# Four GNN layers on one Trainium2 core: a new order on DVE, ACT and GpSimd inside the steps of layers 2 and 3

## What is computed

```python
x = _layernorm(x + L0(x, adj))            # graph convolution with two batch norms
x = _layernorm(x + L1(x, edges))          # attention over 256 edges, 4 heads
x = _layernorm(x + L2(x, adj, adj))       # three weighted convolutions
x = _layernorm(x + L3(x, adj))            # attention over all pairs of nodes

def _slconv(x, adj, S, W):                # layer 2: weighting = adj * adj
    return einsum('nm,bmh->bnh', adj * S, einsum('bnf,fh->bnh', x, W))
# L2: h = relu(slconv(x, W1)); h = relu(slconv(h, W2)); slconv(h, W3)     128 -> 256 -> 512 -> 128

def L3(h, adj):
    Wh = h @ W
    e = (Wh @ a1)[:, :, None] + (Wh @ a2)[:, None, :]
    e = where(e >= 0, e, 0.2 * e)                         # leaky ReLU
    e = where(adj == 0, -inf, e)
    return softmax(e, -1) @ Wh
```

## Time and profile before

| | us |
|---|---|
| median of 3 runs | 638.22 (638.16 to 639.72) |
| the profiled execution | 637.05 |
| its span | 635.1 |
| PE busy | 553.0 (87%) |
| DVE busy | 422.8 (67%) |
| ACT busy | 367.1 (58%) |
| POOL busy | 217.7 (34%) |
| mean granted TensorE clock | 0.93 of 2.4 GHz |

### The profile page before, as it was taken

One profiled execution on the slowest core, in us unless ns is written; L12 is line 12 of the kernel. 1 busy time (PEld: TensorE's weight loads), 2 busy tenths in 40 slices (PEclk: granted clock), 3 DMA queues, 4 the chain that ended last, 5 costly groups with the idle time before them and its releaser, 6 DMA issues.

```text
span 635.1 us, 11295 instructions
## 1 busy us (share of the span) xinstructions
PE 553.0 (87%) x3508; PEld 488.5 (77%) x3508; DVE 422.8 (67%) x1446; ACT 367.1 (58%) x733; POOL 217.7 (34%) x253
## 2 busy tenths in 40 slices
PE   2999797789998799998998999899799799799372
PEld 2888443568886798988988889889789789789262
DVE  5588586788882644685585575675675675755895
ACT  1566692576653245366666666666665765663660
POOL 6840520565663312314215215215215115103231
PEclk9999799699998799999899899799899899799777
DMA  5223000321100000000001001000000000100002
GB/s 178 87 79 99 2 0 0 98 57 45 33 1 0 2 1 1 1 1 1 1 2 35 0 1 33 0 0 23 10 0 12 22 0 1 33 1 9 26 2 66
DMA packets 28382, 15.25 MB, mean 24 GB/s; under 512 B 2320, under 2 KB 28048, under 8 KB 28352
## 3 DMA queue, kind: packets, MB, share of 16 engines
q1 hardware_dynamic: 27792, 13.65, 7.5%
q0 software_dynamic: 560, 1.25, 0.5%
HBM read 10.69 MB, written 4.19 MB: 23 GB/s over the span
## 4 chain that ended last, share of the span: by engine, by line
PE 71%; DVE 12%; ACT 9%; issue 4%; POOL 2%; DMA 1%; SPq 1%; DVEq 0%; ACTq 0%; POOLq 0%
PE psum L237 13%; PE psum L238 12%; PE psum L239 12%; PE psum L1496 8%; PE psum L1321 5%; PE psum L1363 4%; ACT soft L1178 4%; ACT ob L231 3%; PE psum L1448 2%; PE psum L1370 2%; PE psum L1374 2%; PE psum L1384 2%; PE psum L1438 2%; DVE ln_st L183 2%; PE psum L1542 2%
## 5 line engine op out<-in xcount | busy, mean ns | idle before, releaser
L202 POOL TENSOR_TENSOR ln_r<-ln_v,mhalf 128x8 f32<-128x8 f32 x32 | 53.8, 1681 | 257.6 <-DVE ln_v L196 257.6
L1496 PE MATMUL psum<-l2w_s,h 128*128 128x128 f32 x512 | 59.7, 275 | 0.0
L1496 PEld LDWEIGHTS psum<-l2w_s,h 128*128 128x128 f32 x512 | 59.0, 192 | 0.7
L1165 ACT ACTIVATE h<-psum 128x512 f32<-128x512 f32 x64 | 37.3, 596 | 33.4 <-PE psum L239 33.4
L237 PE MATMUL psum<-qt_hi,l2w_s_hi 128*128 128x512 f32 x128 | 52.6, 411 | 0.0
L238 PE MATMUL psum<-qt_lo,l2w_s_hi 128*128 128x512 f32 x128 | 50.5, 394 | 0.0
L239 PE MATMUL psum<-qt_hi,l2w_s_lo 128*128 128x512 f32 x128 | 50.5, 394 | 0.0
L231 ACT ACTIVATE keep_x<-keep_x,ln_b,ln_r (+1 forms) x112 | 45.9, 483 | 1.4 <-POOL ln_b L205 1.4
L854 DVE TENSOR_TENSOR s_lo<-psum,s_hi 128x512 fp32r<-128x512 f32 x16 | 11.1, 692 | 47.5 <-ACT s_hi L1169 47.5
L183 DVE BATCH_NORM_STATS2 ln_st<-keep_x 128x6 f32<-128x128 f32 (+1 forms) x192 | 39.1, 277 | 2.9 <-ACT keep_x L1092 1.6
L237 PE MATMUL psum<-l2w_s_hi,pt_hi 128*128 128x256 f32 x64 | 22.4, 350 | 19.6 <-DVE pt_lo L839 19.6
(11 more groups left out here) (225 smaller groups left out, 1824.9 us busy)
## 6 DMA issues: line engine op xcount, KB each, us to landing
xin<-in_x SPq DMA_DIRECT2D x64, 128.0 KB, 2.2
out_x<-ob SPq DMA_DIRECT2D x32, 128.0 KB, 1.8
l2w_raw<-in_l2w POOLq DMA_DIRECT2D x1, 512.0 KB, 6.7
adjs<-in_adj SPq DMA_DIRECT2D x1, 256.0 KB, 2.7
adjs<-in_adj_t SPq DMA_DIRECT2D x1, 256.0 KB, 2.9
l2w_s<-in_l2w POOLq DMA_DIRECT2D x1, 256.0 KB, 6.5
w_raw<-in_w_t SPq DMA_DIRECT2D x1, 128.0 KB, 3.2
w2t<-in_w_t SPq DMA_DIRECT2D x1, 128.0 KB, 3.2
```

Of the source, the lines that this page charges most:

```text
L202: pool.tensor_tensor(ln.r[:].rearrange("p s k -> p (s k)"), ln.v[:].rearrange("p s k -> p (s k)"), mhalf[:], ALU.pow).then_inc(ln.root, 1)
L1165: act.activation(h2[:, s, g, :], bank(4 + g)[:, 0, :], ACT.Relu).then_inc(h2_out, 1)
L1496: i = pe.matmul(bank(s)[:, 0, k * D:(k + 1) * D], h2[:, s, g, j * N + t * P:j * N + (t + 1) * P], l2w3_s[:, g, :], start=(g == 0), stop=(g ...
```

## The change

No instruction is added or taken away, and PE and SP are untouched. Inside `step`, and in DVE's tail, the order is another:

- POOL: `weigh` comes first, then the roots of ln2 and ln1, then `split_x3(p-1)`, both `split_x(p+1)`, and the root of ln3 last.
- DVE: `variance(p-1, ln2)` moves behind both `h1_low` and the first addition of layer 1; `variance(p+1, ln1)` ahead of `turned_low`; the eight maxima of `scores3` between the two `s3_low`; the three small steps become `highest`, behind the second `s3_low`; both additions of layer 2 follow, and only then `leaky3` of slot 0. `leaky3` of slot 1 comes in the next step, behind both `pt_low`.
- ACT: `exps` moves from ahead of `h1_high` to ahead of `qt_high`; the scalings of ln2 move in between the ReLUs of `h2`; those of ln1 come ahead of the last two ReLUs of slot 1; those of ln3 ahead of `s3_high(p, 1)`.

```diff
             def step(p, two_ahead=True, ahead=True, behind=True, two_behind=True):      # POOL
-                if behind:
-                    ln_power(pool, p - 1, ln2)
                 if two_ahead:
                     for s in range(2):
                         weigh(s, 2 * (p + 2) + s, False)
+                if behind:
+                    ln_power(pool, p - 1, ln2)
                 if ahead:
                     ln_power(pool, p + 1, ln1)
+                if behind:
+                    split_x3(p - 1, not two_behind)
                 if ahead:
                     split_x(p + 1, 0, False)
+                    split_x(p + 1, 1, False)
                 if two_behind:
                     ln_power(pool, p - 2, ln3)
-                if ahead:
-                    split_x(p + 1, 1, False)
-                if behind:
-                    split_x3(p - 1, not two_behind)
...
+            def highest(p):                                                             # DVE
                 dve.wait_ge(tm_done, 2 * p + 2)
...
-            def leaky3(p):
-                for s in range(2):
-                    dve.wait_ge(zt_ready, 2 * p + s + 1)
+            def leaky3(p, s):
+                dve.wait_ge(zt_ready, 2 * p + s + 1)
...
                 for s in range(2):
                     pt_low(p, s)
+                if two_behind:
+                    leaky3(p - 2, 1)
+                for s in range(2):
+                    h1_low(p, s)
+                if ahead:
+                    add(p + 1, 0, o1_done, 4, ln1)
                 if behind:
                     variance(p - 1, ln2, not two_behind)
-                for s in range(2):
-                    h1_low(p, s)
-                for s in range(2):
-                    if ahead:
-                        add(p + 1, s, o1_done, 4 + s, ln1)
-                    qt_low(p, s)
+                qt_low(p, 0)
+                if ahead:
+                    add(p + 1, 1, o1_done, 5, ln1)
+                qt_low(p, 1)
...
+                if ahead:
+                    variance(p + 1, ln1, False)
                 if two_behind:
                     turned_low(p - 2)
                     weights3(p - 2, layer2_first(p))
-                if ahead:
-                    variance(p + 1, ln1, False)
...
+                if behind:
+                    scores3(p - 1)
                 s3_low(p, 1)
                 if behind:
-                    scores3(p - 1)
-                    leaky3(p - 1)
+                    highest(p - 1)
                 for s in range(2):
                     add(p, s, o2_done, 2 + s, ln2)
+                if behind:
+                    leaky3(p - 1, 0)
...
+            leaky3(IT - 2, 1)                                                           # DVE, tail
             variance(IT - 1, ln2, False)
...
             scores3(IT - 1)
+            highest(IT - 1)
             weights3(IT - 2, False)
-            leaky3(IT - 1)
+            for s in range(2):
+                leaky3(IT - 1, s)
...
                 for s in range(2):                                                      # ACT
-                    if two_behind:
-                        exps(p - 2, s)
                     if ahead:
                         y1_turned(p + 1, s, 6 + s)
                     h1_high(p, s)
                 for s in range(2):
+                    if two_behind:
+                        exps(p - 2, s)
                     qt_high(p, s)
-                    if behind:
-                        ln_scale(act, row(p - 1), p - 1, s, ln2)
                 if two_ahead:
                     for s in range(2):
                         weighted_high(p + 2, s, False)
-                for s in range(2):
+                if behind:
+                    ln_scale(act, row(p - 1), p - 1, 0, ln2)
+                for s in range(2):
+                    h2_relu(p, 0, s)
                     if two_behind:
                         turned_exps(p - 2, s)
-                    for g in range(2):
-                        h2_relu(p, 0, 2 * s + g)
+                h2_relu(p, 0, 2)
+                if behind:
+                    ln_scale(act, row(p - 1), p - 1, 1, ln2)
+                h2_relu(p, 0, 3)
...
-                for g in range(2, GB):
-                    h2_relu(p, 1, g)
-                    if ahead and g == 2:
-                        ln_scale(act, row(p + 1), p + 1, 0, ln1)
+                for s in range(2):
+                    if ahead:
+                        ln_scale(act, row(p + 1), p + 1, s, ln1)
+                    h2_relu(p, 1, 2 + s)
                 s3_high(p, 0)
-                if ahead:
-                    ln_scale(act, row(p + 1), p + 1, 1, ln1)
-                s3_high(p, 1)
                 if two_behind:
                     for s in range(2):
                         ln_scale(act, last_sum, p - 2, s, ln3)
+                s3_high(p, 1)
                 if behind:
                     sum_scores(p - 1)
```

More of the change, by code:

```diff
@@ L887, in scores3 @@
                 dve.tensor_scalar(zm[:, 2], zm[:, 1], -1.0, None, ALU.mult).then_inc(m_step, 1)
-            def leaky3(p):
-                for s in range(2):
-                    dve.wait_ge(zt_ready, 2 * p + s + 1)
-                    z = soft[:, s].rearrange("p k n -> p (k n)")
-                    dve.scalar_tensor_tensor(out=z, in0=z, scalar=SLOPE, in1=z, op0=ALU.mult, op1=ALU.max).then_inc(lk_ready, 1)
+            def leaky3(p, s):
+                dve.wait_ge(zt_ready, 2 * p + s + 1)
+                z = soft[:, s].rearrange("p k n -> p (k n)")
+                dve.scalar_tensor_tensor(out=z, in0=z, scalar=SLOPE, in1=z, op0=ALU.mult, op1=ALU.max).then_inc(lk_ready, 1)
             def turned_low(p, slots=(0, 1)):
```

## The result

| | before | changed kernel |
|---|---|---|
| median | 638.19 us (4 runs) | 604.38 us (603.24 to 607.21, 4 runs) |
| ratio | | 0.9473, 95% interval 0.9441 to 0.9505 |
| the profiled execution's span | 635.1 | 601.4 |
| narrow(1) of step 1 to narrow(1) of step 7 | 289.04 to 580.13: 291.1 | 289.30 to 549.00: 259.7 |
| from there to the end of the span (the tail) | 55.0 | 52.4 |

The changed kernel is 5.3% faster. Of 33.7 us between the two spans, 31.4 lie between the two `narrow(1)` and 2.6 in the tail; the stretch ahead of the first of them is 0.25 us longer than before.

What follows compares the result with a forecast made beforehand. PE was taken as the bound, stopped by late `pt_lo` and then slow-clocked. 30.9 + 3.1 - 0.7 - 1.1, less 0.2 in five steps, gave 31.2 us; 637.05 became 605.9, plus 1.2 gave 607.0, range 603 to 616 (forecast alone 603 to 610).

Steps and rivals of the forecast that it cites:

- signs of being wrong: Late `s3_hi` of slot 1, `turn_exps(0)` waiting for `qt_lo`, own_scores above 3.5 us, or slow clock with no gap before it.
- Gaps and clock: Head of steps 2 to 7: PE's waits for `pt_lo` and the slow clock behind them go, 30.9 us gained.
- Thin places: Handovers with little cover, thinnest at ACT's ln3 scalings ahead of `s3_high(p, 1)`: 0.2 us lost in each of five steps.
- Step 1: No attention of layer 3 between its matmuls; ReLUs behind the ln1 and ln2 scalings on ACT run late, 0.7 us lost.
- The second rival: GpSimd's splits of x3 beside `own_scores` hold up DVE, ln3 0.8 us late in five steps: 611 us; chance 0.12.
- Step 7: No `attend1` to cover converting the first `pt` and `h1`; 1.1 us lost, including 0.2 for `pt_lo`.
- Tail: Behind the last step: the application of ln2 starts at 594.9 instead of 598.06, 3.1 us gained.
- no copy of `qt` is late: Exponentials behind `h1_high`, 1.97 us a set, fit ahead of `qt_high(0)` and between the two `qt_high`.
- the strict form: Skill page's rule: two-SBUF-input DVE instructions and SBUF-reading GpSimd instructions exclude each other for the whole instruction.
- No wait stayed: Rival: at the head or `qt_lo(0)`, PE stops about 1 us in each of six steps, clock kept: 613; chance 0.15.
- no clock was lost: Rival: a stop of 1 to 2 us and 1.4 us of slow clock per step give 622; chance 0.05.
- GpSimd's last root: Slower case: four splits queued ahead of ln3's root make it late; splits three times as long give 674; chance 0.04.

Runs made afterwards that it cites:

- the swapped order: Changed kernel with mix_out of slot 1 behind the next step's mix_x of slot 0, and on DVE leaky ReLU of slot 0 between the two additions: 601.3 us.
- both head moves undone: Changed kernel with scalings of ln3 (ACT) behind s3_high of slot 1 and maxima (DVE) behind s3_low of slot 1 again: 618.6 us.
- scalings undone: Changed kernel with the eight scalings of ln3 on ACT behind s3_high of slot 1 again: 616.9 us, ratio 0.9672.
- the last version tried: Version with mix_out swapped, plus GpSimd's order as before the change and, in the tail, own_scores ahead of turned_low of slot 1: 603.4 us.

## Why the prediction was right

**The bound and the gain: right.** The six stops and the slow clock behind them are gone: the clock is 1.00 from 224.4 to 558.9 us, and `pt_hi` waits for PE. One of the prediction's own signs of being wrong did appear, `own_scores` above 3.5 us; see the shared reads below.

**The size: 604.4 measured, 607.0 forecast, in the range.** The terms:

- *Gaps and clock*, forecast 30.9. From `narrow(0)` to `narrow(0)`, steps 1 to 7, the time fell by 3.6, 5.1, 6.3, 5.1, 4.9 and 5.5 us, 30.6 in all. The losses in steps 1 and 7, forecast apart, are already taken off; with them put back (0.74 and 1.2 to 1.3) the term is 32.5 to 32.7, 1.6 to 1.8 more than forecast. Step 3 shows why: 48.77 to 43.63, 5.14, against 3.21 + 1.60 = 4.81 by the list and the windows. A step with a gap is 0.3 us longer than the gap's listed idle time and the slow clock explain, as the experiments with a stop of PE show too (1.77 for 1.54, 1.3 for 0.9, 1.0 for 0.6). Six times 0.3 are 1.8.
- *Thin places*, 0.2 in each of five steps: measured 0. The head of ACT is as thin as the prediction said, with 0.1 us between the last scaling of ln3 and `s3_hi` of slot 1, but it held, and the stop ahead of `mix_out(1)` did not grow (0.23 and 0.24). The earlier trace rows calls that stop PE's; its row is one of the weight loads, and 0.21 us in a step is what the swapped order gained.
- *Step 1*, forecast 0.7: `narrow(0)` to `narrow(1)` took 5.59 instead of 4.85 us, 0.74. The size fits by luck, the cause is another. The prediction named ACT's ReLUs behind the scaling; PE waited 0.52 us, ahead of `spread3`, for `own_scores`, which GpSimd's splits held up. With GpSimd's order undone and ACT's kept, the stretch takes 4.90, so ACT's ReLUs cost 0.05 at most. The second rival's mechanism was at work, in the one step that has no cover for it.
- *Step 7*, forecast 1.1: a stop of 0.94, 1.2 or 1.3 with its unlisted part. Right in place and reason, and `pt_lo` cost 0.15 where 0.2 was allowed.
- *Tail*, forecast 3.1, measured 2.6: the application of ln2 began 15.5 us behind the second `narrow`, not 14.8. The additions and leaky ReLUs end where the layout had them. The time is lost behind them: the exponentials start 0.4 us after the first leaky ReLU has ended, and `ext_hi` waits another 0.16 us for the transposes.
- *Ahead of step 1's `narrow(0)`*, not forecast: 0.5 (284.19 to 283.71).

Against the forecast of 31.2 that is 1.7 more for the gaps, 1.0 more for the thin places, 0.5 more ahead and 0.5 less in the tail, near enough the 33.7 by which the profiled execution is shorter.

**The cover of each move.** The kernel with the variance ahead of `h1_low` again bears out the 0.8 us expected for that place (0.6 listed, 1.0 by the step), that with the leaky ReLUs ahead of the additions the 0.4 to 0.5 expected there (0.3 listed, 0.5 by the step). The prediction's "no copy of `qt` is late" held for the whole change, but it treated exponentials and variance as two independent moves. They aren't: 5.9 alone, 8.2 alone, 8.0 together.

**The rule on the shared reads.** The trace of before had GpSimd's root and `own_scores` side by side with no loss, and I took that against the strict form. With the split beside it the strict form is what the rows show: one `own_scores` instruction lasts 0.69 us beside a 0.69 us cast and one 1.38 beside a 1.36 us subtraction. The Trainium skill's page "SBUF — State Buffer", section "Who interferes with whom", is right for these: DVE's instruction ends 0.14 to 0.16 us after GpSimd's each time. The root of 8 columns (1.64 us) still doesn't hold DVE up, neither in step 4 of the kernel before nor in step 1 of the changed one, where the longest of the `own_scores` instructions beside it takes 0.31 us. The rival priced the delay at 3.8 us of splits and was wrong in that: only the first split meets `own_scores` (1.5 us), since the second waits for `attend3` of slot 1 and starts as `own_scores` ends, and 1.5 us have cover, with 0.76 left over.

**The other rivals.** No wait stayed, no clock was lost, GpSimd's last root had 0.72 us idle ahead of it, the 0.7 of cover that was worked out.

## What to carry to other kernels

When one engine feeds on two others by turns, write the step out against that engine running without a stop, and check for each instruction of the two feeders both who waits for it and what is queued behind it; a move that looks free by the first question can cost by the second, as the exponentials did. Prices of moves on parallel queues don't add (9.4 and 8.5 gave 11.6, 5.9 and 8.2 gave 8.0), so a test that undoes one move alone tells what the rest of the order makes of it, not what it is worth. And a stop of PE's matmuls costs more than its listed idle time: 0.2 to 0.4 us in every run here, and all stops of 2.37 us and more but one cost 1.4 us and more of half clock on top.

## What the runs showed of the hardware

**The clock behind a stop.** All numbers are the listed idle time and the granted clock behind it, in steps 2 to 7. After 0.3 to 1.56 us it stayed at 1.00 each time (50 stops), and after 1.90. Near 2.4 it went either way: 2.37 (before, step 2) and 2.38 (both head moves undone, step 7) lost it, down to 0.50, while 2.48 (scalings undone, step 7) kept it. 3.00 and more lost it each time (8 stops), in the kernel before for 1.4 to 2.8 us of PE's time. The Trainium skill, page "TensorE: Matmul & The Clock Gate", section "HAM oscillation — how this bites in real kernels", advises to keep PE's work free of long gaps; the rows here agree, with that price for each loss. The fall can come late: 1.2 us after the end of the stop of 2.37, and, in the tail of the version with `mix_out` swapped, 1.8 us after that of one of 3.07, behind which eight transposes still ran at 1.00.

**A slower clock can cost more than an earlier start brings.** In the last version tried `spread3` started 1.2 us earlier in the tail, but later one of PE's idle stretches was 2.89 us instead of 1.86, and the 16 transposes behind it took 1.7 us longer, at a granted clock of 0.50 instead of 1.00.

**Shared reads, one instruction at a time.** A DVE instruction with two SBUF operands that takes 0.28 us alone took 0.69 beside GpSimd's cast of 0.69 us and 1.38 beside its subtraction of 1.36 us.
